# VectorE's order in the steps without y: rectified g ahead of the low half of h

## The reference

```python
# layer 0: x rectified, centred, turned by u, clipped, quantised to 8 bits, turned back
im = relu(x) as (256, 32*3136);  mn = mean(im);  p = clip(u.T @ (im - mn), -cv, cv)
p = round((p - dmin) * scale) / scale + dmin;  p = u @ p;  x = p - mean(p) + mn
# layer 1: an attention per image and channel from a covariance
h = relu(bn(w_conv1 @ x));  d = relu(bn(w_dr @ h + b_dr))      # 256 and 128 rows by 3136 columns
xc = d - mean(d);  cov = bn(xc @ xc.T / M)                     # 128 x 128 per image
r = sum over h of w_row[c, j, h] * cov[c, h], plus b_row
att = sigmoid(w_fc @ r + b_fc);  out = x * att
```

## Time and profile before

| what | value |
|---|---|
| median of 3 runs | 1894.13 us (1892.45 to 1895.07) |
| the profiled execution | 1892.99 us, span 1891.2 us |
| TensorE busy | 1672.6 us, 88% of the span |
| VectorE busy | 1536.7 us, 81% |
| ScalarE busy | 1488.9 us, 79% |
| GpSimd busy | 460.3 us, 24%, all in the first stage |
| mean granted TensorE clock | 0.941 |
| DMA | 477.36 MB, mean 252 GB/s |

### The profile page before, as it was taken

One profiled execution on the slowest core, in us unless ns is written; L12 is line 12 of the kernel. 1 busy time (PEld: TensorE's weight loads), 2 busy tenths in 40 slices (PEclk: granted clock), 3 DMA queues, 4 the chain that ended last, 5 costly groups with the idle time before them and its releaser, 6 DMA issues.

```text
span 1891.2 us, 39996 instructions
## 1 busy us (share of the span) xinstructions
PE 1672.6 (88%) x13394; PEld 1316.9 (70%) x13394; DVE 1536.7 (81%) x2813; ACT 1488.9 (79%) x2265; POOL 460.3 (24%) x136
## 2 busy tenths in 40 slices
PE   8999999999992000589999999999999999999998
PEld 8999999999992000366666666666666766766665
DVE  6888888888887755667888888888888888888885
ACT  7777777777769997678888878878888787887885
POOL 7888888888860000000000000000000000000000
PEclk9999999999995555799999999999999999999999
DMA  9998999999999999402545546546455464554635
GB/s 336 371 374 307 375 356 325 370 341 342 373 350 399 429 430 430 169 1 90 207 168 186 204 164 221 171 172 222 158 214 183 155 237 160 199 191 162 233 115 205
DMA packets 140590, 477.36 MB, mean 252 GB/s; under 512 B 10624, under 2 KB 33536, under 8 KB 125568
## 3 DMA queue, kind: packets, MB, share of 16 engines
q1 hardware_dynamic: 140544, 476.75, 68.4%
HBM read 284.04 MB, written 192.68 MB: 252 GB/s over the span
## 4 chain that ended last, share of the span: by engine, by line
PE 56%; ACT 1%; DVE 1%; issue 1%; ACTq 0%; DVEq 0%
PE z_ps L970 18%; PE y_ps L944 17%; PE d_ps L897 14%; PE cov_ps L879 5%; PE ch_ps L955 1%; ACT h L1020 0%; PE ch_ps L910 0%; PE ch_ps L909 0%; ACT hh L1025 0%; DVE g L1185 0%; PE y_ps L926 0%; PE cov_ps L882 0%; DVE hl L1167 0%; PE z_ps L926 0%; PE d_ps L926 0%
## 5 line engine op out<-in xcount | busy, mean ns | idle before, releaser
L299 POOL TENSOR_TENSOR xl<-early,xh 128x1568 fp32r<-128x1568 f32 x128 | 459.4, 3590 | 96.6 <-ACT xh L258 96.6
L1167 DVE TENSOR_TENSOR hl<-h,hh 128x1024 f16<-128x1024 f32 (+2 forms) x224 | 244.1, 1090 | 100.6 <-ACT hh L1025 100.4
L970 PE MATMUL z_ps<-qr,wl 128*128 128x512 f16 (+2 forms) x896 | 315.1, 355 | 0.0
L970 PE MATMUL z_ps<-qr,wh 128*128 128x512 f16 (+2 forms) x896 | 314.9, 355 | 0.0
L944 PE MATMUL y_ps<-qr,udh 128*128 128x512 f16 x868 | 303.7, 353 | 1.8 <-ACT p_res L1054 1.8
L258 ACT ACTIVATE xh<-early 128x1568 fp32r<-128x1568 f32 x128 | 194.1, 1517 | 139.4 <-PE pp L316 139.3
L944 PE MATMUL y_ps<-qr,udl 128*128 128x512 f16 x868 | 303.2, 353 | 0.0
L1054 ACT ACTIVATE p_res<-y_ps,att_cy 128x512 f32<-128x512 f32 x434 | 288.0, 712 | 5.9 <-ACT att_cy L1038 4.3
L1020 ACT ACTIVATE h<-z_ps,sb_h 128x512 f32<-128x512 f32 (+2 forms) x448 | 264.1, 626 | 22.8 <-PE z_ps L970 19.9
L897 PE MATMUL d_ps<-vh,hh 128*128 128x128 f16 x1600 | 280.7, 220 | 1.4 <-DVE hl L1167 1.3
L897 PE MATMUL d_ps<-vh,hl 128*128 128x128 f16 x1600 | 280.7, 220 | 0.0
(11 more groups left out here) (190 smaller groups left out, 2852.6 us busy)
## 6 DMA issues: line engine op xcount, KB each, us to landing
early<-in_x_dram SPq DMA_DIRECT2D x128, 784.0 KB, 6.9
out_dram<-p_res SPq DMA_DIRECT2D x31, 3136.0 KB, 10.2
early<-p_scratch SPq DMA_DIRECT2D x42, 1568.0 KB, 12.7
p_res<-p_scratch SPq DMA_DIRECT2D x112, 512.0 KB, 4.2
p_scratch<-early SPq DMA_DIRECT2D x56, 784.0 KB, 7.8
p_scratch<-late SPq DMA_DIRECT2D x56, 784.0 KB, 7.8
p_res<-p_scratch SPq DMA_DIRECT2D x56, 384.0 KB, 3.2
late_tile<-p_scratch SPq DMA_DIRECT2D x13, 1568.0 KB, 12.8
```

What stands on the lines that cost most here:

```text
L299: nc.gpsimd.tensor_tensor(xl[:, k % 2], xs[:, k], xh[:, k % 2].bitcast(F32), ALU.subtract).then_inc(split_done, 1)
L970: last = nc.tensor.matmul(z_ps[:, m, 0:w], part[:, k, m * P:(m + 1) * P], qr[:, a, k, columns(s)], start=k == 0 and part is wh, stop=k == ...
L1167: nc.vector.tensor_tensor(hl[:, par, :, 0:w], h32[:, par, :, 0:w], hh[:, par, :, 0:w], ALU.subtract).then_inc(h_split, 1)
```

## The change

In the steps that make no y, VectorE issues the rectified g of chunk s - 1 first and the low half of h of chunk s behind it; in all other steps the order stays as it was. Both operations become functions of their own, unchanged in their operands, waits and increments.

```diff
+            def has_no_y(r2, a, s):
+
+                return not has(r2, a, s, CH + Y_LAG)
...
+                def low_half_of_h(r2, a, s):
+                    g, par = first_chunk(r2, a) + s, (CH * a + s) % 2
+                    if exists(r2, a):
+                        w = widths[s]
+
+                        dve.wait_ge(hh_done, g + 1)
+                        nc.vector.tensor_tensor(hl[:, par, :, 0:w], h32[:, par, :, 0:w], hh[:, par, :, 0:w],
+                                                ALU.subtract).then_inc(h_split, 1)
+
+                def rectified_g(r2, a, s):
+                    g, par = first_chunk(r2, a) + s, (CH * a + s) % 2
+                    if has(r2, a, s, 1):
+
+                        dw = widths[(s - 1) % CH]
+                        dt, dq = -(-dw // P), min(P, dw)
+                        dve.wait_ge(d_done, g)
+
+                        wait_from(dve, g_split, g - 1)
+                        nc.vector.scalar_tensor_tensor(out=g32[0:dq, 0:dt], in0=d_ps[0:dq, 1 - par, 0:dt],
+                                                       scalar=1.0 / LIFT, in1=nb[0:dq, 0:dt], op0=ALU.mult,
+                                                       op1=ALU.max).then_inc(d_read, 1)
...
+                        if has_no_y(r2, a, s):
+                            rectified_g(r2, a, s)
+                            low_half_of_h(r2, a, s)
+                        else:
+                            low_half_of_h(r2, a, s)
...
+                            rectified_g(r2, a, s)
```

More of the change, by code:

```diff
@@ L1162, in phase @@
                                     op0=ALU.mult, op1=ALU.add).then_inc(weighted_done, 1)
[L1163 to L1187, removed]
+                        if has_no_y(r2, a, s):
[3 more added lines that the diff above has]
+                            low_half_of_h(r2, a, s)
+                            if has(r2, a, s, CH + Y_LAG) and final(output_chunk(r2, a, s)[0]):
+                                o, slot, c = output_chunk(r2, a, s)
+                                if c == 0:
+                                    dve.wait_ge(attb_done, N)
+                                    dve.wait_ge(out_stored[slot], 16 * (N // 2))
+                                dve.wait_ge(y_done, K * (o) + 2)
+                                nc.vector.tensor_scalar(yo[:, slot, 1, columns(c)], final_ps[c % 3][:, 1, 0:widths[c]],
+                                                        att_cy[:, 1, 0:1], att_cy[:, 1, 1:2], ALU.mult,
+                                                        ALU.add).then_inc(half_free[1], 1)
+                            rectified_g(r2, a, s)
```

## The result

| | before | after |
|---|---|---|
| first comparison, median | 1891.89 us (6 runs) | 1881.27 us (6 runs, 1880.48 to 1882.96) |
| ratio, with its 95% interval | | 0.9943 [0.9932, 0.9955] |
| the profiled execution | 1892.99 us, span 1891.2 us | 1882.96 us, span 1881.2 us |

A forecast was written before the change was run, and what follows sets the result against it. Early steps were bound by a chain of waits through VectorE and ScalarE, later ones by TensorE. Of 12.05 us lost early, 2.82 stay, so 9.23 off the median 1894.13 gives 1884.9 us (-0.49%); range 1882.1 to 1889.2.

The forecast's parts named there:

- The ring: Early steps ahead of 840 us: g, gg, h, hh, hl, next g follow each other, 4.76 us from g to g.
- TensorE's pace and the new ring's room: Early 512-wide steps after the swap: TensorE needs 3.62 us, the chain d, g, hl, d 3.41, leaving 0.21.
- The residual waits: TensorE waits left after the swap at six places in images 0 and 1, summing to 2.82 us.
- The half clock: Fall from 2.4 to 1.2 GHz at 814 to 816 us behind TensorE's long wait, slowing d and z; 1.8 us.
- the 12.05: Microseconds TensorE loses in the early stretch of twelve steps: 56.42 taken less 44.37 of work.
- The gain: Early stretch: 12.05 us lost less 2.82 still waited, 9.23 us, all handed on to the end.
- (a): Early steps: longer handovers let the new d, g, hl chain pace, TensorE waiting 0.2 to 0.5 us each; chance 0.12.
- (b): Early steps: hl behind g makes every d late by 0.60 us, +6.0 us, 1900.1; chance 0.03.
- (c): Before 840 us: time given back at the y wait, result within 0.2% of 1894.1 us; chance 0.04.
- (d): Early steps: VectorE paces, each operation holding the next until its pipe empties; time near 1894 us; chance 0.02.
- from the median, 1884.9 us: Whole kernel: the 9.23 us taken off the runs' median of 1894.13 us, -0.49%.
- No wait of TensorE at all: 12.05, 1882.1: Early stretch: the best case, where all 12.05 us lost there are gained, giving 1882.1 us.

## Why the prediction was right in its steps and wrong in its range

- **The ring** (4.76 us a step through hl, though gg does not need it): right. A longer g lengthens the old step by its whole 0.60 us.
- **TensorE's pace and the new ring's room** (3.62 against 3.41): right. A 512-wide step with no wait in it took 3.62 us, and with g doubled 4.03.
- **The residual waits**: 2.82 us were worked out, and 47.19 - 44.37 = 2.82 came. The six places are those named: 0.35 was worked out for the first (0.19 + 0.16 measured), 0.22 for step 4 (the d at 793.27 comes 1.53 us behind its z, 1.30 without a wait: 0.23), 0.17 for step 5 (the d of 384 columns takes 1.16 us to the covariance, 1.00 without a wait: 0.16), 0.61 for the covariance (0.45 + 0.16), 0.88 for step 3 (0.69 + 0.16), 0.59 for the second y (0.38 + 0.16). These six make 2.74.
- **The half clock**: 1.8 us of the 12.05 were put down to it. It costs 1.2: d and z are slowed by about 1.7 us, but TensorE then waits less further on (z to z of step 3 takes 3.90 us with the fall, 4.34 without). The sum is not touched, as the 12.05 hold it either way.
- **The gain** of 9.23 us: right for the stretch, 9.2 us in the first pair of profiles and 8.9 to 9.3 over all pairs; the second digit is luck. Handed on whole: right, the saturated part is unchanged.
- **The rivals**: (a) was not there: in the stretch hl costs TensorE time in three steps (0.35, 0.23 and 0.85 us) and not in every one. (b) and (c) fell with the gain. (d) fell because VectorE started hl 0.61 us behind a g of 0.69 and lost nothing. Its estimate of 5.5 us comes to 5.2 with the conversion at the 0.55 us of the earlier trace rows, and the sum of VectorE's four spacings to 2.8 instead of 2.96; neither changes the argument. The section that (d) cites (the Trainium skill, "VectorE: DVE Perf Modes", section "The DRAIN you can't avoid") also says that a next operation which is not held starts earlier, and with that exception the trace agrees.
- **The step that failed** is the last one, "from the median, 1884.9 us", with the bound "No wait of TensorE at all: 12.05, 1882.1". It took the median of three runs, 1894.13, as a base without error. Over 82 runs the kernel before has 1891.3; the three had been 2.8 us high, as much as the distance from the forecast to the range's end. From 1891.3 the same gain gives 1882.1, 0.7 us from the changed kernel's 1881.4 over 16 runs. Part of the scatter is the clock's: z of step 0 to z of step 2 takes 7.9 or 10.1 us by when the granted clock rises, and the first z itself came between 774.2 and 777.7 us in the profiles without extra products ahead of it. The range held the unknown costs of the change but not what the base and the start of the stage add to either side. The three comparisons give 10.6, 8.1 and 8.9 us, 9.2 in the mean; that the excess in the first is the same scatter and nothing else is argued from these, not shown run by run.

## What to carry to other kernels

Where the chain of waits runs through an operation whose result the next link does not need, only the order on one engine has put it there; moving it cost little here, as the new ring, with its handovers, stays under the pace of the busiest engine in most steps, and where it does not, the wait could be summed from start-to-start spacings to a few hundredths of a microsecond. The same order was wrong in the steps where d came late (18.6 us), so the condition on the step is part of the change. A forecast of a time needs a base, and with three runs that scatter by 2.6 us the range has to hold that scatter as well.

## What the runs showed of the hardware

- A wait of TensorE of 2.2 us at step 1 of image 1 was followed by 1.2 GHz in all three profiles of the kernel before, and so were 2.2 and 2.7 us there in two other kernels with the old order. It was not once it was filled (two profiles), nor where a swap in one image had cut it to 1.6 or 1.1 us. In the tail the same wait of 1.83 us stands in all fifteen profiles without extra products there: the fall followed in seven (the kernel before in all three, among others) and not in eight (the changed kernel in all three, but also the kernel before with the 24 products in image 1, some 1060 us earlier). What decides between the two there is open.
- The part behind the stretch took 1049.1 to 1050.3 us in every kernel without extra products on TensorE (those with the swap in all steps left out) and 1047.9 to 1048.3 in all six with them, wherever these stood, and with the clock's fall in the tail or without. The steady images are alike in both (34.02 to 34.11 us each). The 2 us are those in which the DMA share stands at 0.06 to 0.07 at the very end, 1.3 to 2.3 us in the twelve profiles without extra products and none in the six with them. From the last output to the span's end it is 4.1 to 4.2 us with them against 5.3 to 6.3 without, where the clock did not fall. What extra products have to do with stores stays open.
- With TensorE busy up to the stage and the clock at 2.4 GHz, the clock fell to 1.2 GHz in the stage's first 3 to 5 us in two of three profiles, though TensorE had work in most of that time (1.05 to 2.00 of each 2 us), products of one column among it.
- At the stage's start TensorE works without a pause from its first product (between 772.5 and 774.9 us) on. The granted clock rose to 2.4 GHz 4.8 to 4.9 us behind that product in three profiles (one of the kernel before, two of the changed one) and 10.7 to 11.0 us behind it in the three others (two and one). That is the short and the long start; what decides between them is open.
